# Routed experts' products in f32 with unsplit operands, in place of three f16 products of upper parts and rests

## The reference

```python
q = (xn @ w_q.T)                      # xn: x normed over its features, then over the tokens
sim = einsum('pbnhd,hkpd->bnhk..', q, keys)      # 8 heads, 2 sides, 64 keys a side
# top 8 a side, the 8 best of their 64 sums: 8 experts of 4096 for each head
o = einsum('bnd,bnhkd->bnhk', inputs, key_in[idx])
o = gelu(o) * softmax(scores)
out = einsum('bnhk,bnhkd->bnd', o, key_out[idx])
```

## Time and profile before

| | us |
|---|---|
| median of 3 runs | 3398.86 |
| the profiled execution | 3402.41 |
| its span, first to last instruction | 3400.6 |
| TensorE matmuls busy (PE) | 3180.5 |
| TensorE weight loads busy (PEld) | 2235.4 |
| VectorE busy (DVE) | 2876.6 |
| ScalarE busy (ACT) | 1644.9 |
| GpSimd busy (POOL) | 677.0 |

### The profile page before, as it was taken

The page is one execution under the profiler, slowest core; times in us unless marked ns, Lnnn a source line. Parts: engine busy times, 40 slices in busy tenths (PEclk is TensorE's granted clock), DMA queues, the critical chain, the costliest instruction groups (busy, mean ns, idle before and its releaser), DMA issues. The chain is left out here.

```text
span 3400.6 us, 74937 instructions
## 1 busy us (share of the span) xinstructions
PE 3180.5 (94%) x29442; PEld 2235.4 (66%) x29442; DVE 2876.6 (85%) x8980; ACT 1644.9 (48%) x2256; POOL 677.0 (20%) x357
## 2 busy tenths in 40 slices
PE   8998799999999988799999999998789999999997
PEld 7886588888888867333333333334568888888886
DVE  5757899999999996788888888882799999999996
ACT  4534444444444434346556656565344444444441
POOL 0000233333333340200000000000033333333333
PEclk9998999999999999799999999998899999999999
DMA  4225000000000005631212111003300000000000
GB/s 154 80 60 161 10 15 11 20 11 20 11 20 11 17 8 167 166 64 34 37 33 51 34 34 36 8 6 113 102 8 11 20 11 20 11 20 11 20 8 17
DMA packets 130869, 140.56 MB, mean 41 GB/s; under 512 B 29974, under 2 KB 115926, under 8 KB 130518
## 3 DMA queue, kind: packets, MB, share of 16 engines
q1 hardware_dynamic: 120918, 126.72, 14.1%
q10 hardware_dynamic: 9600, 9.05, 0.9%
HBM read 84.75 MB, written 50.59 MB: 40 GB/s over the span
## 5 line engine op out<-in xcount | busy, mean ns | idle before, releaser
L490 PE MATMUL f_p_route<-f_x_w,f_y_hot 128*128 128x64 f16 x8192 | 902.4, 194 | 54.1 <-DVE f_weighted L768 42.9
L514 PE MATMUL f_p_out<-kout_in,f_hidden 128*128 128x256 f16 x6144 | 853.7, 273 | 17.5 <-POOL f_hidden L408 16.5
L503 PE MATMUL f_p_hid<-f_xtc,kin_in 128*128 128x256 f16 x6144 | 856.0, 274 | 5.9 <-ACT f_hidden L604 5.8
L408 POOL TENSOR_TENSOR f_hidden<-f_weighted,f_hidden 128x1024 f16<-128x1024 f32 x256 | 612.5, 2393 | 1217.4 <-DVE f_x_w L758 1213.2
L2066 DVE TENSOR_REDUCE at_part_max<-at_p_ring 128x1 f32<-128x512 f32 (+3 forms) x1280 | 706.1, 603 | 113.0 <-PE at_p_ring L1945 74.8
L490 PEld LDWEIGHTS f_p_route<-f_x_w,f_y_hot 128*128 128x128 f16 x8192 | 697.2, 98 | 96.2 <-issue 60.9
L514 PEld LDWEIGHTS f_p_out<-kout_in,f_hidden 128*128 128x128 f16 x6144 | 600.0, 98 | 196.0 <-issue 118.6
L503 PEld LDWEIGHTS f_p_hid<-f_xtc,kin_in 128*128 128x128 f16 x6144 | 602.4, 98 | 80.0 <-issue 10.1
L609 ACT CAST f_hidden<-f_weighted 128x1024 f16<-128x1024 f32 x256 | 342.9, 1340 | 465.3 <-DVE f_weighted L768 465.3
L604 ACT ACTIVATE f_hidden<-f_p_hid 128x512 f32<-128x512 f32 x512 | 301.9, 596 | 500.5 <-PE f_p_hid L503 497.3
L1945 PE MATMUL at_p_ring<-at_k,at_q 96*128 96x512 bf16 (+3 forms) x1280 | 416.3, 362 | 40.0 <-DVE at_m_rest L2083 15.4
(11 more groups left out here) (272 smaller groups left out, 3451.1 us busy)
## 6 DMA issues: line engine op xcount, KB each, us to landing
at_q<-qk SPq DMA_DIRECT2D x42, 256.0 KB, 4.5
at_k<-qk SPq DMA_DIRECT2D x42, 256.0 KB, 4.3
x<-f_ln_y SPq DMA_DIRECT2D x32, 256.0 KB, 2.8
xt<-f_ln_xt SPq DMA_DIRECT2D x32, 256.0 KB, 3.6
f_xt_in<-xt SPq DMA_DIRECT2D x32, 256.0 KB, 2.8
f_xres<-x SPq DMA_DIRECT2D x32, 256.0 KB, 2.7
qk<-ap_parts_q SPq DMA_DIRECT2D x16, 384.0 KB, 3.8
qk<-ap_parts_k SPq DMA_DIRECT2D x16, 384.0 KB, 5.0
```

The costliest lines, as they stand in the source:

```text
L408: nc.gpsimd.tensor_tensor(lo, weighted[s % WR], hi, ALU.subtract).then_inc(lo_ready, 1)
L490: last = nc.tensor.matmul(p_route[:, t, :], y_hot[:, s % HR, t // PAIR, :, t % PAIR], x_w[:, s % HR, half, t // PAIR, :, t % PAIR], start= ...
L503: last = nc.tensor.matmul(p_hid[g % 2][:, xp % 2, :], kin_t[:, a, dh, xp * P:(xp + 1) * P], xt[slot][:, b, dh, :], start=i % 6 == 0, stop= ...
L514: last = nc.tensor.matmul(p_out[:, u, :], parts[slot][:, xp, u * P:(u + 1) * P, a], kout[:, b, xp, :], start=g == 0 and i == 0, stop=xp == ...
```

## The change

The three f16 products become one f32 product. `kin_t`, `kout`, the inputs and the weighted values are f32 and unsplit, in the same bytes as the two f16 parts took. EXPERT_STEPS is 4 in place of 12: one product follows every fourth route product. `weigh` writes its product over `hidden`; `round_weighted`, `split_weighted`, `copy_xt` and `split_xt` are gone, and with them all that GpSimd did in the steps. The inputs are loaded into a ring of three f32 tiles that TensorE and ScalarE read as they come. Where the weights are prepared, key_out is loaded straight to where it stays, and ScalarE copies the transposed key_in once. The scale of 16 stays on the routing weights alone.

```diff
-HR, WR = 2, 2
+HR, XR = 2, 3
...
-        xt = [sb(f"xtc{b}", [P, 2, DH, CH], F16) for b in range(2)]
+        xt = [xt_in] + [sb(f"xtc{b}", [P, DH, CH]) for b in range(XR - 1)]
...
-            def split_weighted(c, slot, s):
-                pool.wait_ge(hi_ready, ONE + c * NS + s + 1)
-                if s + 2 < NS or s + 1 < NS and exists(c + 1):
-
-                    pool.wait_ge(hot_ready, ONE + c * NS + s + 3)
-                hi, lo = step_parts(slot, s)
-                nc.gpsimd.tensor_tensor(lo, weighted[s % WR], hi, ALU.subtract).then_inc(lo_ready, 1)
...
             def load_xt(c):
-
-                above(sp, xt_lo_ready, c)
-                sp.dma_start(xt_in[:], xt_dram[bass.ds(c, 1), :, :, :].rearrange("c p h t -> (c p) h t")).then_inc(xt_loaded, 16)
+                above(sp, xt_loaded, 16 * c if c > 1 else 0)
+                above(sp, hid_ready, (c - XR + 1) * NG)
+                sp.dma_start(xt[c % XR][:], xt_dram[bass.ds(c, 1), :, :, :].rearrange("c p h t -> (c p) h t")).then_inc(xt_loaded, 16)
...
-            EXPERT_STEPS = 12
+            EXPERT_STEPS = 4
 
             def expert_in(c, slot, g, i):
                 if i == 0:
                     if g == 0:
-                        pe.wait_ge(xt_lo_ready, ONE + c + 1)
+                        pe.wait_ge(xt_loaded, ONE + c * 16 + 16)
                     above(pe, gelu_ready, c * NG + g - 1)
-                xp, dh, (a, b) = 2 * g + i // 6, i % 6 // 3, PAIRS[i % 3]
-                last = nc.tensor.matmul(p_hid[g % 2][:, xp % 2, :], kin_t[:, a, dh, xp * P:(xp + 1) * P], xt[slot][:, b, dh, :],
-                                        start=i % 6 == 0, stop=i % 6 == 5)
+                xp, dh = 2 * g + i // DH, i % DH
+                last = nc.tensor.matmul(p_hid[g % 2][:, xp % 2, :], kin_t[:, dh, xp * P:(xp + 1) * P], xt[c % XR][:, dh, :],
+                                        start=dh == 0, stop=dh == DH - 1)
...
             def expert_out(c, slot, g, i):
                 if i == 0 and g == 0:
-                    pe.wait_ge(lo_ready, ONE + c * NS + NS)
+                    pe.wait_ge(routed, ONE + c * NS + NS)
 
                     above(pe, y_ready, c)
-                xp, u, (a, b) = 2 * g + i // 6, i % 6 // 3, PAIRS[i % 3]
-                last = nc.tensor.matmul(p_out[:, u, :], parts[slot][:, xp, u * P:(u + 1) * P, a], kout[:, b, xp, :],
-                                        start=g == 0 and i == 0, stop=xp == NX - 1 and i % 3 == 2,
+                xp, u = 2 * g + i // 2, i % 2
+                last = nc.tensor.matmul(p_out[:, u, :], hidden[slot][:, xp, u * P:(u + 1) * P], kout[:, xp, :],
+                                        start=g == 0 and i == 0, stop=xp == NX - 1,
                                         skip_group_check=True)
...
-                            for i in range(j % PS * 3 // 4, (j % PS + 1) * 3 // 4):
+                            for i in range(j % PS // 4, (j % PS + 1) // 4):
                                 do(*at, i)
...
-            def round_weighted(c, slot, s):
-                act.wait_ge(routed, ONE + c * NS + s + 1)
-                hi, lo = step_parts(slot, s)
-                nc.scalar.copy(hi, weighted[s % WR]).then_inc(hi_ready, 1)
...
-                above(dve, lo_ready, c * NS + s + 1 - WR)
                 h = hidden[slot][:].rearrange("p x (u t) -> p x u t", u=2)[:, :, :, s * PS:(s + 1) * PS]
-                nc.vector.tensor_tensor(weighted[s % WR], h, p_route[:].rearrange("p t (u x) -> p x u t", u=2),
+                nc.vector.tensor_tensor(h, h, p_route[:].rearrange("p t (u x) -> p x u t", u=2),
                                         ALU.mult).then_inc(routed, 1)
...
             def load_kout(j):
-                above(sp, kout_lo, j - SLOTS + 1)
-                sp.dma_start(kout[j % SLOTS][:], key_out.rearrange("(x y) d -> y x d", y=P)[:, j * XG:(j + 1) * XG, :]).then_inc(
-                    kout_loaded[j % SLOTS], 16)
+                sp.dma_start(kout_t[:, j * XG:(j + 1) * XG, :], key_out.rearrange("(x y) d -> y x d", y=P)[:, j * XG:(j + 1) * XG, :]).then_inc(
+                    kout_loaded, 16)
...
-                    nc.scalar.mul(kin_home(i, 0), p_prep[:], E_SCALE).then_inc(kin_hi, 1)
+                    nc.scalar.copy(kin_home(i), p_prep[:]).then_inc(prep_taken, 1)
...
-                elif FIRST_KIN <= n < N_PREP:
-                    i = kin_item(n)
-                    dve.wait_ge(kin_hi, ONE + i + 1)
-                    nc.vector.scalar_tensor_tensor(kin_home(i, 1), p_prep[:], E_SCALE, kin_home(i, 0),
-                                                   ALU.mult, ALU.subtract).then_inc(prep_taken, 1)
...
-            def rest_of_kout(j):
-                dve.wait_ge(kout_hi, ONE + j + 1)
-                nc.vector.scalar_tensor_tensor(kout_home(j, 1), kout[j % SLOTS][:], E_SCALE, kout_home(j, 0),
-                                               ALU.mult, ALU.subtract).then_inc(kout_lo, 1)
```

More of the change, by code:

```diff
@@ L566, in normalise @@
                 for dh in range(DH):
-                    last = nc.scalar.activation(xn[:, dh, :], xt_in[:, dh, :], ACT.Identity,
+                    last = nc.scalar.activation(xn[:, dh, :], xt[c % XR][:, dh, :], ACT.Identity,
                                                 bias=shift[:, dh:dh + 1], scale=scale[:, dh:dh + 1])
                 last.then_inc(xn_ready, 1)
-            def copy_xt(c, slot):
-                above(act, hid_ready, (c - 1) * NG)
-                nc.scalar.copy(xt[slot][:, 0, :, :], xt_in[:]).then_inc(xt_copied, 1)
             def copy_scores(c, u):
@@ L603, in gelu @@
                 above(act, out_read, (c - 2) * NG + g + 1 if not isinstance(c, int) or c > 1 else 0)
-                nc.scalar.activation(hidden[slot][:, 2 * g:2 * g + 2, :], p_hid[g % 2][:], ACT.Gelu, scale=1.0 / E_SCALE).then_inc(gelu_ready, 1)
-            def round_weighted(c, slot, s):
-                act.wait_ge(routed, ONE + c * NS + s + 1)
-                hi, lo = step_parts(slot, s)
-                nc.scalar.copy(hi, weighted[s % WR]).then_inc(hi_ready, 1)
+                nc.scalar.activation(hidden[slot][:, 2 * g:2 * g + 2, :], p_hid[g % 2][:], ACT.Gelu).then_inc(gelu_ready, 1)
             def one(c, slot):
@@ L619, in one @@
                         normalise(c + 2)
-                        copy_xt(c + 2, slot)
                     if s == EXP_AT and nxt:
@@ L626, in one @@
                         copy_picks(c + 1, 1 - slot)
-                    round_weighted(c, slot, s)
                     if s == PAIR_AT and nxt:
@@ L774, in add_residual @@
                 nc.vector.scalar_tensor_tensor(xres[:].rearrange("p u d -> p (u d)"), p_out[:].rearrange("p u d -> p (u d)"),
-                                               1.0 / E_SCALE ** 2, xres[:].rearrange("p u d -> p (u d)"), ALU.mult, ALU.add).then_inc(y_ready, 1)
+                                               1.0 / E_SCALE, xres[:].rearrange("p u d -> p (u d)"), ALU.mult, ALU.add).then_inc(y_ready, 1)
             def one(c, slot):
@@ L893, in memory_gradients @@
         keys_t = sb("keys_t", [P, NH, NK, 2])
-        kin, kout = ring("kin", [P, XG, D], SLOTS), ring("kout", [P, XG, D], SLOTS)
+        kin, wq_rows = ring("kin", [P, XG, D], SLOTS), sb("wq_rows", [P, DH, D])
         p_prep = pb("prep")
-        keys_loaded, prep_ready, prep_taken, kin_hi = (sem("mg_" + n) for n in ("keys_loaded", "prep_ready", "prep_taken", "kin_hi"))
-        kout_hi, kout_lo = sem("mg_kout_hi"), sem("mg_kout_lo")
-        kin_loaded, kout_loaded = ([sem(f"mg_{n}{i}") for i in range(SLOTS)] for n in ("kin_loaded", "kout_loaded"))
+        keys_loaded, prep_ready, prep_taken, kout_loaded = (sem("mg_" + n) for n in ("keys_loaded", "prep_ready", "prep_taken", "kout_loaded"))
+        kin_loaded = [sem(f"mg_kin_loaded{i}") for i in range(SLOTS)]
         natural = {"W0": kin[0][:, 0:DH, :], "Wk": w["Wk"], "Wv": kin[0][:, DH:2 * DH, :], "W1": w["W1"], "Wout": kin[1][:, 0:DH, :]}
@@ L1008, in _ @@
                 sp.wait_ge(xt_stored[b], ONE + 16 * len(range(b, NCH, RT)))
+            sp.wait_ge(kout_loaded, ONE + 16 * N_KOUT)
             sp.wait_ge(s["xln_ready"], ONE + NCH)
@@ L1156, in _ @@
             pe.wait_ge(us["loaded"], ONE + 16 * (NGATE + 1))
-            products(p_first, wq_rows, w0n).then_inc(us["first_ready"], 1)
+            products(p_first, wq_rows[:], w0n).then_inc(us["first_ready"], 1)
         @block.scalar
@@ L1213, in step @@
                     prepare(n - 5)
-                    if kout_item(n - 5) is not None:
-                        round_kout(kout_item(n - 5))
                 if valid(n + 2):
@@ L1298, in step @@
                     prepare(n - 5)
-                    if kout_item(n - 5) is not None:
-                        rest_of_kout(kout_item(n - 5))
                 if n % 2 == 0 and 0 <= n // 2 + 2 < NCH:
@@ L2234 @@
 LATER_OF_EXPERTS = """
-iota_ready xn_ready xt2_copied sim_ready sim_copied sim_used best_ready exp_ready keys_paired picks_ready picks_turned
```

(5 more changed lines are left out.)

41 lines of the change are left out of this document (7 added, 34 removed).

## The result

The changed kernel took 3883.44 us, the median of four runs (3882.69 to 3883.77), against 3398.88 us before in the same comparison: 1.1423 times as long, 95% interval 1.1404 to 1.1443. The prediction was 3887 us.

The account below looks back on a forecast made before the run. TensorE was taken as full and the bound, VectorE nearly level. Middle chunks 456, chunk 14 20 and the stretch ahead of chunk 0 12 sum to 488 us, giving 3887 us against the median; range 3810 to 3940.

Parts of the forecast that it names:

- The bound, and the product: Middle chunks: TensorE is full; an f32 product costs 0.432 us for three f16 products' 0.327, +13.4 us a chunk.
- The weight load behind a route product: Expert products behind route products: 0.083 us of the first f32 load lies open, +5.3 us a middle chunk.
- B: Rival at route products: the f32 load is hidden there as well, 148 us less, 3739 us; chance 9%.
- C: Rival at route products: more than one load is open, 148 us more, 4035 us; chance 8%.
- D: Rival: TensorE gets cheaper, an f32 product's two records overlapping; DVE's 55.05 us then bounds, about 3295 us; chance 3%.
- The 1.1 us a chunk of handovers: Middle chunks: TensorE's 1.1 us a chunk of handovers with DVE goes, as DVE's 55 us lie inside the longer chunk.
- Chunk 0, priced at 0: Chunk 0: PE's 47.3 us stays under DVE's 54.4, so the change there is hidden by DVE, 0 us.
- Ahead of chunk 0: Stretch before chunk 0, where expert_in(0) runs by itself on the path: +5.9 us a stage, +12 us.
- Chunk 15 and the end, priced at 0: From chunk 15's first weigh to the last product: 62.5 us before and after, 0 us.

Follow-up runs that it names:

- experiments 1 and 2: The changed kernel with its f32 products among the routes in pairs, 3805.18 us; then with all four of a half step in a row, 3771.61 us.
- experiment 11: The kernel before with one f16 product in place of three and nothing split (weighted values written in f16, no rounding or subtractions in routed_experts): 3250.56 us.
- experiment 6: The kernel before with one f16 product in place of three, the vector work unchanged: 3333.24 us.
- Experiment 9: The changed kernel with ScalarE's rounding put back in each step, into a spare tile nobody reads, GpSimd still empty: 3887.72 us in one run.
- experiment 10: The kernel before with ScalarE's copy of the scores at steps 3 and 7 ahead of the same step's rounding: 3401.47 us.
- experiments 1 to 4: Besides experiments 1 and 2: the changed kernel with one more VectorE comparison a step, 3906.98 us; and the change for the first product alone, 3629.21 us.

## Why the prediction was right

**The bound, and the product.** Right. TensorE was full and VectorE just behind it. The product cost 0.432 us, as in the f32 rows of the first stage, and the three f16 products gave back 0.109 each. In the middle chunks 452.7 us came where 456 were forecast.

**The weight load behind a route product.** Right, and shown by taking the cause away in two doses: 0.0825 and 0.081 us a load, where the prediction took 0.083 from the distance of loads behind three-column products. In the changed kernel these slots are 64 x 0.082 = 5.2 of the 17.4 us a middle chunk. B and C are excluded by experiments 1 and 2. D fell with the 0.432; its bound, VectorE's 55.05 us, was found in experiment 11 at 55.05 and in experiment 6, with the splits in place, at 57.02.

**The 1.1 us a chunk of handovers.** Right in size, and right only in part as to whose they are: a third is VectorE's. Steps 2 to 5 of a chunk take 7.07 us each from score product to score product, as the prices give. The excess stands in four places of steps 6, 7 and 0, where a product starts later than its price after the one before. On average over the 13 middle chunks of the first stage these are:

- 0.4 us before the score product of step 0, and 0.1 before its second record: TensorE waits for the inputs of chunk c+2 that ScalarE norms;
- 0.23 us before the first route product of step 7, which waits for VectorE's `weigh` of step 6;
- 0.2 us before the first `expert_out` of a chunk, which waits for GpSimd's last subtraction;
- 0.15 us before the transposes, which wait for VectorE's picks.

The rest, some 0.2 us, is spread over the transposes and all other slots. The profile marks only the longest of these as waits, since the records of pipelined products overlap the others. PE before the change, 500 to 1100 us:

```profile
PE f_p_sim L471 <- ACT f_xn L567: 2.8, 4, 1.8
```

The ends of the `weigh` (762.84) and of the subtraction (772.03), and the products behind them:

```profile
761.62 1.22 DVE L768 TENSOR_TENSOR f_weighted<-f_hidden,f_p_route 128x1024 f32<-128x1024 f32 x1
762.99 0.22 PE L490 MATMUL f_p_route<-f_x_w,f_y_hot 128*128 128x64 f16 x2
767.21 4.82 POOL L408 TENSOR_TENSOR f_hidden<-f_weighted,f_hidden 128x1024 f16<-128x1024 f32 x2 [2.97 <-DVE f_x_w L758]
772.08 0.28 PE L514 MATMUL f_p_out<-kout_in,f_hidden 128*128 128x256 f16 x1
```

The sum held, because all of them went under the longer chunk, as assumed: PE waits for nothing in a middle chunk after.

**Chunk 0, priced at 0.** Wrong in size: between the first `weigh`s it became 2.9 and 2.5 us shorter. The step that failed is "0, hidden by DVE; without that cover it would be what exceeds 57.6". It looked only at what TensorE gains in work, and took DVE's pace there as fixed, although gave it 3.2 idle us. I asked whether ScalarE's removed work was hidden beside PE, and not what is queued behind it on ScalarE: the copy of the scores, for which VectorE waited 2.28 us. Experiment 9 gives 1.65 us of chunk 0 back with the rounding alone, and experiment 10 takes the wait away in the kernel before. GpSimd's collisions make 0.55 us more. How much of the 5.4 us the span gained by it isn't shown: in experiment 9 chunk 1 made good for all of the 1.65 us.

**Ahead of chunk 0.** Right: +4.7 in the trace of the change, where the first `weigh` of the kernels with the same f32 `expert_in(0)` came between 374.5 and 375.1 us (experiments 1 to 4), and at 369.07 before. Kernels with the same f16 `expert_in(0)` differ among themselves by up to 1.9 us there (367.20 in experiment 10).

**Chunk 15 and the end, priced at 0.** Off by 2.4 us in the second stage. The wait of `expert_out(15)` for `routed` is short, as said, but it also waits for `y_ready`, VectorE's `add_residual` of chunk 14. TensorE's last rows:

```profile
3847.83 0.59 PE L482 MATMUL f_p_out<-kout_in,f_hidden 128*128 128x256 f32 x2
3849.30 27.86 PE L482 MATMUL f_p_out<-kout_in,f_hidden 128*128 128x256 f32 x128 [0.88 <-DVE f_xres L727]
```

Before, GpSimd's subtraction came later and covered it. When a wait goes, the next in line on the same instruction takes over, and I had not priced it. With it the time from the last `weigh` to the last 64 products is 2.6 us, where the sum has 1.7. Another 0.9 us are the steps of chunk 15, the first of 5.19 us and six of 4.82 where seven of 4.75 were summed. The rest lies in the last products and behind them.

**The errors together.** The two profiles differ by 481.2 us where 488 were summed. Chunk 0 (5.4 us), the middle chunks (3.3) and smaller terms (1.8) came out shorter than forecast, the end (2.4) and the stretch between the stages (1.5) longer. So the errors only partly cancel, and that the medians lie within 4 us of the forecast (3883.44 against 3887) owes something to that.

## What to carry to other kernels

Splitting f32 operands into two f16 parts and making three products was worth it here: 3 x 0.109 us against 0.432, plus 0.08 us wherever the f32 product follows a short one. If f32 products must stand among short f16 ones, put them in a row, so that each covers the next one's load (112 us here). Work that a change removes from another engine bought nothing beside a full TensorE; where that engine's queue is on the path, look at what stands behind the removed work. And count what two engines need before taking work off one: with TensorE at 57.9 us and VectorE's chain at 57.0, leaving out two thirds of the expert products moved a middle chunk by 0.9 us.

## What was unexpected of the hardware

An f16 product of 64 columns with its own 128-column weight load costs 0.030 us in a row of 16, while four f32 loads in a row came at 0.113 us each: product and load together take less than a third of one f32 load. The Trainium skill ("TensorE: Matmul & The Clock Gate", Weight-path perf modes) states that the fast load, which is on for types other than FP32, is measured at about twice the speed. Here an f16 load comes at least 3.7 times as fast as an f32 load, and the measurement decides; no run here has an f16 load without the fast path.

With a third of the expert products TensorE's granted clock fell. A window of chunk 8 in experiment 6:

```profile
833.00:891.00 58.00, 41.31 (x409) 28.27 (x409) 55.84 (x201) 27.18 (x37) 20.23 (x9) 0.78 0.05 15
```

PE was busy 41 of 58 us, in spells with waits for VectorE between them, and the mean clock was 0.78 of 2.4 GHz, where it was 1.00 before the change. What TensorE waited for most in chunks 1 to 12 of this kernel (us in total, times, longest):

```profile
PE f_p_route L490 <- DVE f_weighted L768: 182.5, 78, 4.7
```

The lower clock cost nothing in the middle chunks there, since VectorE waited for no product. What it would cost with TensorE on the path, no run here shows.
